# Every gelu remainder on VectorE out of PSUM, and a new order on three engines, in a fused attention and routed-layer kernel

## What is computed

```python
def block1(x):                       # x: (2, 2048, 256)
    z = layernorm(x)
    q, k, v = [gelu(z @ W1 + b1) @ W2 + b2 for (W1, b1, W2, b2) in (Q, K, V)]
    s = tril(q @ k.T / sqrt(256 * 512))           # no softmax: a linear, causal attention
    return layernorm(s @ v) * ln_w + ln_b

def block2(z):                       # z: layernorm of x + block1
    idx = argmax(pe @ sign(tile_sigs).T, axis=-1) # one of 8 tiles for each position
    return z @ W[idx].T + b[idx]

x = x + block1(x)
out = x + block2(layernorm(x))
```

## Time and profile before

| | us |
|---|---|
| runs shown | 330.68 median of 3 (329.66 to 331.28) |
| the profiled execution's own time | 329.83 |
| its span (first to last instruction) | 328.1 |
| busy: PE, PE weight loads | 281.4 (86%), 252.1 (77%) |
| busy: DVE, ACT, POOL | 232.0 (71%), 202.5 (62%), 196.8 (60%) |

### The profile page before, as it was taken

How to read it: one execution, slowest core, us unless ns; L and a number is a source line. 1 busy time by engine, 2 the same in 40 slices (tenths; PEclk the granted TensorE clock), 3 DMA queues, 4 the chain that set the end, 5 groups by cost and what they waited for, 6 DMA issues and landing times.

```text
span 328.1 us, 5585 instructions
## 1 busy us (share of the span) xinstructions
PE 281.4 (86%) x1828; PEld 252.1 (77%) x1828; DVE 232.0 (71%) x538; ACT 202.5 (62%) x402; POOL 196.8 (60%) x227
## 2 busy tenths in 40 slices
PE   5899999799989998899899999999998969996000
PEld 5778988698779888787878898899887969996000
DVE  3799759778987768865876787679569798885000
ACT  2377576667566884587468856966774469991000
POOL 3533506451664787589638854964793557777772
PEclk9579999999999999999999999999999999999555
DMA  8806940200020012001201040100047414943210
GB/s 213 284 0 212 337 156 1 67 31 0 2 91 8 32 65 98 32 33 34 97 2 47 20 128 16 51 1 2 32 122 193 125 53 137 306 145 112 75 54 2
DMA packets 24656, 28.01 MB, mean 85 GB/s; under 512 B 4722, under 2 KB 22386, under 8 KB 24564
## 3 DMA queue, kind: packets, MB, share of 16 engines
q1 hardware_dynamic: 15764, 13.07, 13.6%
q0 software_dynamic: 3488, 8.99, 7.8%
q10 hardware_dynamic: 5376, 5.59, 5.4%
HBM read 13.99 MB, written 14.56 MB: 87 GB/s over the span
## 4 chain that ended last, share of the span: by engine, by line
PE 63%; DVE 17%; POOL 5%; issue 5%; ACT 5%; DMA 3%; POOLq 0%; SPq 0%; DVEq 0%; ACTq 0%
PE ring L427 35%; PE o_ps L427 9%; PE s_ps L427 6%; POOL out_dram L1477 5%; PE sc_ps L427 4%; DMA w_stage<-w1k 3%; PE w_ps L427 2%; DVE xres L1004 2%; PE ring L440 2%; PE ring L669 2%; PE ring L518 1%; DVE hT L930 1%; DVE state L976 1%; DVE kT L942 1%; DVE v L955 1%
## 5 line engine op out<-in xcount | busy, mean ns | idle before, releaser
L427 PE MATMUL ring<-xnT,w_sp 128*128 128x512 f32 x288 | 75.1, 408 | 3.1 <-DVE xnT L925 1.7
L427 PEld LDWEIGHTS ring<-xnT,w_sp 128*128 128x128 f32 x288 | 54.0, 195 | 15.6 <-issue 2.0
L427 PE MATMUL ring<-hT,w_sp 128*128 128x512 f32 x192 | 47.4, 398 | 4.5 <-DVE qT L936 3.0
L726 ACT ACTIVATE h<-ring,b_cols 128x512 f32<-128x512 f32 x48 | 33.0, 687 | 21.1 <-PE ring L427 20.7
L427 PEld LDWEIGHTS ring<-hT,w_sp 128*128 128x128 f32 x192 | 35.0, 188 | 14.2 <-DVE qT L936 4.1
L1392 POOL DMA_INDIRECT sorted_rows<-xres,slot_i x32 | 33.8, 1057 | 8.6 <-issue 6.1
L1356 POOL TENSOR_TENSOR hT<-h,hT 128x512 fp32r<-128x512 f32 x24 | 31.7, 1331 | 4.5 <-ACT hT L729 4.3
L1362 POOL TENSOR_TENSOR vtok<-v,vtok 128x512 fp32r<-128x512 f32 x14 | 17.7, 1284 | 23.8 <-ACT vtok L749 23.8
L1381 POOL TENSOR_TENSOR xres<-ve,half 128x4 f32<-128x4 f32 (+1 forms) x9 | 8.7, 968 | 37.2 <-DVE ve L1024 37.1
L729 ACT CAST hT<-h 128x512 fp32r<-128x512 f32 x48 | 29.8, 620 | 1.5
L976 DVE TENSOR_TENSOR state<-s_ps,state 128x512 fp32r<-128x512 f32 x27 | 18.6, 688 | 16.5 <-ACT state L768 16.5
(11 more groups left out here) (181 smaller groups left out, 635.8 us busy)
## 6 DMA issues: line engine op xcount, KB each, us to landing
sorted_rows<-blank ACTq DMA_DIRECT2D x1, 5070.0 KB, 20.3
xt<-x SPq DMA_DIRECT2D x8, 512.0 KB, 3.6
slot_rows<-sorted_rows SPq DMA_DIRECT2D x23, 130.0 KB, 4.0
h<-sorted_rows SPq DMA_DIRECT2D x16, 130.0 KB, 2.7
w_stage<-tile_w SPq DMA_DIRECT2D x8, 256.0 KB, 4.0
hT<-position_table POOLq DMA_DIRECT2D x1, 512.0 KB, 7.1
sorted_rows<-xres,slot_i POOLq DMA_INDIRECT x32, 2.7
row_stage<-rows ACTq DMA_DIRECT2D x1, 384.0 KB, 8.1
```

The costliest lines, as they stand in the source:

```text
L427: last = te.matmul(o, lhs[k][a], rhs[k][c], start=start and k == 0 and i == 0, stop=stop and k == n - 1 and i == 2, skip_group_check=check)
L726: nc.scalar.activation(h32[:, m, :], ring[(2 + m) % 3][:, :], ACT.Gelu, bias=b1c[:, m // 2, m % 2:m % 2 + 1]).then_inc(gelu, 1)
```

## The change

Six things change.

1. Gelu on ACT writes back into its own PSUM bank instead of h32, and the rounding copy reads that bank. All six remainders of a step are made on DVE, out of PSUM. POOL makes none.
2. A bank is free for PE only when DVE has made the remainder from it (bank_free), not when gelu has read it.
3. The remainder of k is made from PSUM (bias added in the same instruction, as q's is) instead of from the SBUF copy k32; the two PE waits on k_full become waits on k_lo. The masked scores stay in PSUM in all steps but the last.
4. On DVE the order in a body is new: remainders 0 and 1 come first, with the statistics x1_stats and x1_var of the body before between and behind them; the two small instructions behind each aggregation (negated mean, variance plus eps) move to POOL.
5. On POOL, residual(s + 1) moves from near the end of a body to its start, rstd_lead stands ahead of rstd_x1, and step 0's rows are sent in body 1 (in the loop of s = 1, which is while step 2's front is made) instead of body 2.
6. On ACT, the normalisation of the next rows is spread over the body, and q's rounding follows out_squared directly.

The core of the diff:

```diff
@@ PE @@
+            def bank_free(s, m):
+                te.wait_ge(h_lo_dve, PARTS * s + m + 1)
...
                     if m >= 3:
-                        te.wait_ge(gelu, 6 * s + m - 2)
+                        bank_free(s, m - 3)
...
-                te.wait_ge(h_lo_dve, len(DVE_H) * s + sum(m < 2 * which + 2 for m in DVE_H))
-                te.wait_ge(h_lo_pool, len(POOL_H) * s + sum(m < 2 * which + 2 for m in POOL_H))
+                te.wait_ge(h_lo_dve, PARTS * s + 2 * which + 2)
...
                     if j < 3:
-                        te.wait_ge(gelu, 6 * s + 4 + j)
+                        bank_free(s, 3 + j)
...
-                        te.wait_ge(k_full, 2 * s + 1)
+                        te.wait_ge(k_lo, 2 * s + 1)
@@ ACT @@
-                nc.scalar.activation(h32[:, m, :], ring[(2 + m) % 3][:, :], ACT.Gelu,
+                full = ring[(2 + m) % 3][:, :]
+                nc.scalar.activation(full, ring[(2 + m) % 3][:, :], ACT.Gelu,
                                      bias=b1c[:, m // 2, m % 2:m % 2 + 1]).then_inc(gelu, 1)
                 act.wait_ge(gelu, 6 * s + m + 1)
-                nc.scalar.copy(hT[:, m, 0, :], h32[:, m, :]).then_inc(h_hi, 1)
+                nc.scalar.copy(hT[:, m, 0, :], full).then_inc(h_hi, 1)
...
-                if s + 2 < STEPS:
-                    lead_norm(s + 2, (0, 1))
                 hidden(s + 1, 4)
-                out_squared(s, 2)
+                if s + 2 < STEPS:
+                    lead_norm(s + 2, (0,))
                 hidden(s + 1, 5)
@@ DVE @@
             def h_rest(s, m):
                 dve.wait_ge(h_hi, 6 * s + m + 1)
-                nc.vector.tensor_tensor(hT[:, m, 1, :], h32[:, m, :], hT[:, m, 0, :].bitcast(F32),
+                nc.vector.tensor_tensor(hT[:, m, 1, :], ring[(2 + m) % 3][:, :], hT[:, m, 0, :].bitcast(F32),
                                         ALU.subtract).then_inc(h_lo_dve, 1)
...
-                nc.vector.tensor_tensor(kT[:, 1, j, :], k32[:, j, :], kT[:, 0, j, :].bitcast(F32),
-                                        ALU.subtract).then_inc(k_lo, 1)
+                nc.vector.scalar_tensor_tensor(out=kT[:, 1, j, :], in0=ring[(10 + j) % 3][:, :],
+                                               scalar=b2c[:, K, j:j + 1], in1=kT[:, 0, j, :].bitcast(F32),
+                                               op0=ALU.add, op1=ALU.subtract).then_inc(k_lo, 1)
...
             h_rest(0, 0)
+            h_rest(0, 1)
             route_argmax()
             h_rest(0, 2)
+            h_rest(0, 3)
             weights_rest((5,))
             h_rest(0, 4)
+            h_rest(0, 5)
@@ POOL @@
             def rstd_lead(s):
+                pool.wait_ge(aggr1, s + 1)
+                nc.gpsimd.tensor_scalar(nm1[:, :], mv1[:, :, 0], -1.0, None, ALU.mult)
+                nc.gpsimd.tensor_tensor(ve1[:, :], mv1[:, :, 1], eps[:, :], ALU.add).then_inc(var1, 1)
...
             for s in range(LAST):
+                residual(s + 1)
+                if s + 2 < STEPS:
+                    rstd_lead(s + 2)
+                if s:
+                    rstd_x1(s - 1)
+                if s > 1:
+                    rows_sorted(s - 1, (0, 1))
+                if s == 3:
+                    tile_shifted(4)
+                rstd_out(s)
...
```

142 lines of the change are left out of this document (64 added, 78 removed).

## The result

The changed kernel takes 326.61 us (median of 4 runs, 325.87 to 327.64), the kernel before 330.17 in the same session (329.53 to 331.28): 3.6 us less, ratio 0.9891 with a 95% interval of 0.9849 to 0.9933. The profiled execution took 326.29 (span 324.5), against 329.83 (328.1). First the windows by body of the changed kernel, with the borders where PE begins the transposes of the next step's front; they answer to the earlier trace rows, and the columns are the same.

What follows compares the result with a forecast made beforehand. PE was taken to wait in bodies 0 to 3, mostly for DVE, which POOL holds up where both inputs are in SBUF. Terms +1.2 - 1.9 - 0.4 - 1.4 + 3.2 - 0.1 - 0.3 = +0.3 gave 330.1, or 331.0 against the median (329.3 to 332.7).

Steps and rivals of the forecast that it cites:

- Start: Before the loop: PE waits for banks behind remainders 0 and 2, and remainder 5 delays q's remainder; +1.2 us.
- Body 0: Body 0: route_order loses 1.8 of POOL stretch, q's first remainder ends at 20.8 instead of 23.1; -1.9 us.
- body 2: Body 2: with the residual early, v's sum is never late and the body goes to 29.4; -1.4 us.
- Body 1: Body 1: new 1.4 wait for remainder 2, but route_slots 1.8 shorter and q's remainder earlier; body takes 31.4, -0.4 us.
- Body 3: Body 3: POOL's new order makes tile 4 late, PE waits 5 to 6 us, later small waits go; +3.2 us.
- Bodies 4 to 6 and the end: Bodies already at PE's work, -0.1; last body's x1_final and DVE chain to the first slot shorter, -0.3 us.
- PSUM as the source: DVE remainders: reading PSUM takes 0.68 us, as from SBUF, against the Trainium skill's about 65 ns more per instruction.
- (a): Rival, body 3: the wait for tile 4 is small because h5 covers most of it; 328.3 us, chance 0.20.
- (b): Rival, bodies 0 and 1: DVE becomes the bound, routing instructions being long of themselves; 335.0 us, chance 0.08.
- (c): Rival, six bodies: x1_final(3) and the state's remainder wait for residual, a bank late by 0.4; 333.4 us, chance 0.12.
- (d): Rival: stretches move to other two-input instructions, gains of bodies 0 to 2 halve; 332.9 us, chance 0.12.

Runs made afterwards that it cites:

- E3: Changed kernel plus two unneeded POOL subtractions of two SBUF inputs, behind the lead's rstd in bodies 0 and 1: 330.24 us.
- E7: E1 with remainders 1, 3 and 5 on POOL, from SBUF: +1.62, +0.79 and +0.47 us in bodies 0 to 2, against E1.
- E14: E1 with ACT's order of the kernel before: 3.45 us slower, 1.34 in body 0 and 2.23 in body 1.
- E16: E15 with POOL's whole loop as in the kernel before, only tile 4 early: bodies 0 to 2 sum to 94.2 us, against 93.8 in the kernel before.
- E9: E1 with the residual directly behind rstd_out again, the step's row DMAs ahead of rstd_out: 321.40 us, against 320.85 for E1 repeated on the same chip.
- E15: E1 with both E7's remainders on POOL and E14's ACT order: bodies 0 to 2 sum to 90.8 us, against 87.8 in E1.
- E1: Changed kernel, but in body 3 POOL prepares tile 4 right behind the residual: 320.00 us.
- E2: Changed kernel with gelu, rounding and remainders through SBUF, PE needing only gelu to take a bank again: 326.56 us.
- E8: E1 with DVE's start reordered (remainder 0 ahead of the statistics, remainder 2 ahead of the argmax): 319.58 us, against 320.85 for E1 repeated, same chip.
- E5: E1 with E2's edit (gelu, rounding and remainders through SBUF): ratio 0.967 to the kernel before.
- E3b: As E3, but the extra POOL instructions add a constant to one SBUF input: 326.82 us.

## Why the prediction was wrong

The sum was 330.1 for the profiled execution; it took 326.3. Between the medians the miss is 4.4 (331.0 and 326.6), since the profiled execution lies 0.3 under its median this time and not 0.85. Step by step:

- Start, +1.2: against PE's first product it was 24.95 instead of 23.6, +1.3, with the bank waits for remainders 0 and 2. Right, by its mechanism: remainder 0 ended 7.7 us and remainder 2 11.0 us behind the first product, where I had 7.6 and 11.0. PE's wait for remainder 0 reads 1.76 and not 0.4, because its first three products were done after 5.98 us, not 7.18, at a granted clock of 0.72 against 0.58. But the first product came at 12.95 instead of 14.08 us. In the kernels above it comes between 12.4 and 14.9, so I take the 1.1 us between the two profiles for chance; what fixes this moment was not tested.
- Body 0, -1.9, was -2.4; body 2, -1.4, was -1.8. The mechanism of the first is shown (E3, E7), but not as the only one: by E14 ACT's order is needed as well, 1.3 us. In body 2 POOL's order is what counts (E16, 3.4 us); the residual's place alone is worth 0.8 (E9).
- **Body 1, -0.4, was -1.8: this is the step that failed.** I had remainder 2 end at 15.0 in the body and h5 wait 1.4 for it; it ended at 14.25, h4 was done at 13.9 instead of 13.6, and h5 waited 0.44. That is 1.0 of the 1.4 us. The likely reason is arithmetic: DVE's rows overlap, and durations add up to too much. Remainder 2 lasts 0.67 from 80.27, and the next instruction starts at 80.86. The 11 rows from 71.09 to 80.27 add up to 9.8 us of durations in 9.2 us, nearly all of the 0.75 by which I had remainder 2 too late. The other 0.4 lies behind it: q's first remainder ended at 21.8 instead of 23.0. It was 1.0 early by remainder 4 already (19.0 instead of 20.0). Behind that, two moves in the diff that no step of my sum named nearly cancel: ACT no longer has its pair of normalisations, 1.0 us, in front of q, and the centring now stands behind remainder 5, 0.6 later. I had put ACT's order at nothing without a reason; its price in this body is 2.2 us by E14 and 0.8 by E15 against E7.
- Body 3, +3.2, was +3.4, but of other parts: the tile came 20.3 into the body and not 21.6, PE waited 4.48 and not 5 to 6, and the clock behind it cost 1.7, which my sum left out. E1 confirms both. The tile 1.3 us sooner and the slow clock nearly cancel: that 3.2 came so near to 3.4 is in part luck.
- Bodies 4 to 6 and the end, -0.4, were -1.1: behind the last body the wait for the first slot's normalisation was 0.44 instead of 1.49. DVE's four x1 instructions in front of it take 1.66, and the remainder before them 0.69 instead of 1.52; that this is the cause is my reading.
- PSUM as the source at no cost per instruction: right (684 ns). The Trainium skill (Perfetto Trace Analysis, Optimizing Scalar/DVE Operations) gives about 65 ns more to each, which for 48 remainders would be, as an estimate, 3.1 us more of DVE's time; E2's, from SBUF, took 704 ns, 20 more and not 65 less.

Errors of 1.4 (body 1), 1.1 (arrival), 0.7 (end), 0.5 and 0.4, all to one side, outweigh 0.2 in body 3: 3.8 us. Of my rivals, (a) came nearest, 328.3, still 1.7 too high, and by a mechanism that did not occur, since the wait for tile 4 was there. (b) is out, since the routing instructions take 0.2; (c), since PE waited for no state; (d), since bodies 0 to 2 gained 6.0 and not half of 3.7.

What stays open is the exact share of each part: their effects do not add, so they can only be told in an order of undoing. No run undoes the masked scores in PSUM, the small statistics on POOL or the order of DVE's remainders by itself.

## What to carry to other kernels

The gains of several moves need not add: undoing one of two parts here cost 2.9 or 3.6 us in bodies 0 to 2, undoing both 3.0. Follow the waiting instruction back on every engine that feeds it before pricing a move, and go through every moved line of the diff, the harmless ones too. An instruction that fits into a gap of its queue should stand in that gap: tile 4 behind the residual instead of behind two row DMAs was worth 6.1 us, E8, with it and the reordered start, is 3% faster than the kernel before, and the change alone 1%. For a hand schedule take the distances between the starts of rows, not their durations.

## What the runs showed of the hardware

- A wait of PE costs more than its length when the clock falls behind it: 4.48 us of waiting were 6.13 us of time, and in E2 5.51 were 7.8 (37.13 against 29.35 in E5). In E3 a wait of 1.77 in body 1, with another of 0.63 some 7 us before it, was followed by a granted clock of 0.57; the 1.76 and 0.25 in the start of the changed kernel were followed by 1.00.
- DVE and POOL hold each other up in both directions: DVE's 0.18 became 1.17 behind a two-input subtraction of POOL (E3), POOL's power went from 1.04 to 1.46 and its row DMAs from 1.12 and 0.98 to 1.38 and 1.27 beside two-SBUF-input remainders of DVE (E2). With one input on POOL's side it was 0.36 (E3b). A DVE copy of one SBUF input went from 0.17 to 1.19 beside POOL's subtractions (E7).
- On ACT, gelu from PSUM into PSUM took 660 ns on average and the rounding out of PSUM 587, against 687 and 621 with SBUF in between (E2).
